# A decoder layer's opening redrawn, later quarter sums moved two steps, and weight halves kept in DRAM

## The chip, the core and the metric

The kernel runs on one core of one Trainium2 chip. The time is the device time in microseconds (us) of one execution, launch to end; the figures are medians of a few runs.

The engines: TensorE (PE) multiplies matrices, VectorE (DVE) and GpSimd (POOL) do elementwise work and sums, ScalarE (ACT) does copies, squares and exponentials, and SyncE (SP) issues nearly all DMAs, one after the other, in an order written out by hand. Each engine has its own instruction stream; semaphores tie them.

## The reference

One decoder layer on x (4 x 256 x 512) with a context of 4 x 1601 x 512, in float32:

```python
x = layernorm(x + self_attn(x))        # attention over the 16 positions inside a row, 8 groups
x = layernorm(x + cross_attn(x, ctx))  # 32 heads, 8 key heads, head size 128, 1857 keys
x = layernorm(x + ffn(x))              # router softmax over 64 experts, the top 8, expert biases

# self_attn: for each of the 1024 rows by itself
q, k, v = x @ Wq + bq, x @ Wk + bk, x @ Wv + bv      # (16, 32), (16, 8), (16, 8)
out[d, h] = sum_e softmax_e(sum_h q[d, h] k[e, h // 4] / 4) v[e, h // 4]

# cross_attn: kv = concat([ctx, x]); q and k are RMS-normed and scaled by a learned weight
p = softmax(q @ k.T / sqrt(128)); out = concat_heads(p @ v) @ Wo
```

## The kernel before

**Cross-attention.** There are 4 batches and 8 key heads, so 32 units (`UNITS`, batch-major). A unit has two halves: 512 query columns (2 heads of 256 rows) against 15 key tiles (`NJ`) of 128 keys. A *step* is one key tile of one half; a unit is a *cycle* of 30 steps (`CYCLE`). Products of which float32 accuracy is wanted are made of three passes over operands split in a high and a low part (`three`, L772 to L774): a weight chunk comes into `w_stage` by DMA, ACT copies the high part (`split` of ACT, L1184), and POOL subtracts it from the chunk for the low part (`split` of POOL, L746). Each unit needs five chunks of 128 x 1024: `Wkv`, `Wq` twice and `Wo` twice. They depend on the key head alone, so each batch does the same splits over again. `splits(s)` says at which step a chunk is split; `weights(chunk)` on SP loads a chunk two steps after the chunk two places ahead of it was split, and waits for that split's semaphore `s_wl`.

All engines walk through the same steps in the order of `for s in STEPS`, each in its own stream. At step s PE does the scores of tile s, then the *fill* jobs of that step, then P V of tile s - 20. Fill jobs: X turns a row tile of keys (transpose; ACT and DVE write its two halves, SP stores it in `kvT_scratch`), KV projects a key tile with `Wkv`, Q projects queries, KT and QT turn keys and queries, MT, AT and RB serve maxima and sums, O multiplies by `Wo`. DVE keeps the running maximum (L1364), which the scores of two steps on wait for, shifts the scores (L1348), and drains the jobs. ACT copies scores (L1047) and takes exponentials (L1060, L1061), and POOL writes `P_lo` (L689) and adds the probabilities up (L707). A negative step number is the opening, whose jobs stand in the table `OPENING`; the first scores are step 0.

**Self-attention.** Its 1024 rows are 8 tiles. PE turns and projects all eight in the opening (`SELF_AT`: "turn", "project"; L878, L889, L890). Tiles 0 and 1 are finished there, since batch 0's queries and last keys need their result (X 0 and X 1). The products are made in four quarters, quarter 0 by DVE and 1 to 3 by POOL (L459, L466), and summed by DVE (L1247, L1274). Tiles 0 and 1 go through five stages, "products", "scores", "normalise", "residual", "layernorm", both tiles at the same step one after the other, so DVE does a stage for tile 0 and at once for tile 1. Tiles 2 to 7 are kept in DRAM and finished later (`LATER`): each has 14 events, three in every 15 steps. At an event POOL makes one quarter's products in the one buffer `self_products`, and DVE sums that quarter at the end of the step after it (L1299 for q k, L1317 for p v), in its own order behind the other work of the step. The next quarter's product waits until the sum is done. The last of these tiles ends in unit 14 of 32.

**Order in the opening.** PE at a step: scores, fill jobs, then the self-attention's turn and projection, then P V. ACT likewise does the self-attention's copies last. SP loads one key row tile ahead of two weight chunks at the start.

## Time and profile before

| | |
|---|---|
| median of 3 runs | 2921.55 us (2919.27 to 2922.64) |
| the profiled execution | 2920.32 us, of which the span from first to last instruction 2918.5 |
| PE busy | 2791.9 us (96% of the span) |
| POOL busy | 2428.4 us (83%) |
| DVE, ACT busy | 2164.7 us (74%), 2066.0 us (71%) |
| mean granted PE clock | 0.978 |
| DMA | 364.81 MB, 125 GB/s |

### The profile page before, as it was taken

The numbers are of one execution on the slowest core, as the hardware profiler recorded it, in microseconds if no ns is written. First come the engines' busy times: TensorE is split into PE (matmuls) and PEld (weight loads), VectorE is DVE, ScalarE is ACT, GpSimd is POOL, SyncE is SP. The second block draws the span as 40 slices with busy tenths as digits, with TensorE's granted clock in tenths as the row PEclk, the third lists the DMA queues.
The fourth block names the chain that finished last, engine by engine and source line by source line (L and its number), as shares of the span: only waits on it lengthen the run. The fifth ranks groups of instructions, "written<-read, shape, count | busy, mean of one in ns | idle before, by whom it ended". The sixth has DMA issues, their size and how long they took to land. (4 is left out here: it accounts for less than half of the span.)

```text
span 2918.5 us, 46903 instructions
## 1 busy us (share of the span) xinstructions
PE 2791.9 (96%) x14860; PEld 2228.7 (76%) x14860; DVE 2164.7 (74%) x3483; ACT 2066.0 (71%) x3867; POOL 2428.4 (83%) x2283
## 2 busy tenths in 40 slices
PE   6999999999999999999999999999999999999976
PEld 4767787777777777778888888888888888888744
DVE  4667787777787778777777777777777777777755
ACT  3666777777676777777777777777777777777741
POOL 4488899889888999898888888888888888888880
PEclk9999999999999999999999999999999999999985
DMA  5633443333343434343444434334334333333201
GB/s 194 202 116 116 137 138 127 133 128 120 126 137 131 140 120 139 124 132 127 135 141 141 133 125 151 127 129 131 131 113 140 105 127 113 110 115 105 65 8 69
DMA packets 155604, 364.81 MB, mean 125 GB/s; under 512 B 12761, under 2 KB 48091, under 8 KB 155360
## 3 DMA queue, kind: packets, MB, share of 16 engines
q1 hardware_dynamic: 153608, 359.98, 37.1%
q8 instruction: 121, 1.98, 0.3%
q10 hardware_dynamic: 1752, 1.84, 0.2%
q14 instruction: 123, 1.01, 0.1%
HBM read 323.89 MB, written 37.88 MB: 124 GB/s over the span
## 5 line engine op out<-in xcount | busy, mean ns | idle before, releaser
L707 POOL TENSOR_TENSOR acc<-acc,scores 128x512 f32<-128x512 f32 (+1 forms) x832 | 1110.3, 1334 | 92.0 <-ACT scores L1061 51.8
L1364 DVE SCALAR_TENSOR_TENSOR running_max<-S_ps,rk,running_max 128x512 f32<-128x512 f32 (+1 forms) x896 | 668.8, 746 | 222.7 <-ACT scores L1047 216.6
L689 POOL TENSOR_TENSOR P_lo<-scores,P_hi 128x512 fp32r<-128x512 f32 x512 | 674.6, 1318 | 168.2 <-ACT scores L1061 168.0
L1047 ACT ACTIVATE scores<-S_ps,rk 128x512 f32<-128x512 f32 (+1 forms) x960 | 652.1, 679 | 200.9 <-PE S_ps L774 194.6
L1348 DVE TENSOR_TENSOR scores<-scores,Mb_ps 128x512 f32<-128x512 f32 (+1 forms) x960 | 648.4, 676 | 163.1 <-PE Mb_ps L922 163.1
L1061 ACT ACTIVATE scores<-scores 128x512 f32<-128x512 f32 (+1 forms) x960 | 596.6, 622 | 72.8 <-DVE scores L1348 71.7
L772 PE MATMUL S_ps<-QT_hi,KT_hi 128*128 128x512 f32 (+1 forms) x960 | 552.6, 576 | 27.0 <-DVE running_max L1364 24.0
L1060 ACT ACTIVATE P_hi<-scores 128x512 fp32r<-128x512 f32 x512 | 321.3, 628 | 263.8 <-DVE scores L1348 240.7
L774 PE MATMUL K_ps<-Wkv_hi,kvT 128*128 128x256 f32 (+1 forms) x1664 | 471.4, 283 | 0.0
L772 PE MATMUL K_ps<-Wkv_hi,kvT 128*128 128x256 f32 (+1 forms) x1664 | 470.6, 283 | 0.0
L773 PE MATMUL K_ps<-Wkv_lo,kvT 128*128 128x256 f32 (+1 forms) x1664 | 470.5, 283 | 0.0
L802 PE MATMUL OT_ps<-scores,V_full 128*128 128x512 f32 (+1 forms) x896 | 466.7, 603 | 0.0
L774 PE MATMUL S_ps<-QT_hi,KT_lo 128*128 128x512 f32 (+1 forms) x960 | 379.4, 395 | 0.0
L773 PE MATMUL S_ps<-QT_lo,KT_hi 128*128 128x512 f32 (+1 forms) x960 | 377.9, 394 | 0.0
L773 PEld LDWEIGHTS K_ps<-Wkv_lo,kvT 128*128 128x128 f32 (+1 forms) x1664 | 309.5, 186 | 19.5 <-issue 0.4
L772 PEld LDWEIGHTS K_ps<-Wkv_hi,kvT 128*128 128x128 f32 (+1 forms) x1664 | 309.3, 186 | 19.8 <-issue 0.5
L772 PEld LDWEIGHTS S_ps<-QT_hi,KT_hi 128*128 128x128 f32 (+1 forms) x960 | 178.0, 185 | 176.5 <-DVE running_max L1364 80.5
L774 PEld LDWEIGHTS K_ps<-Wkv_hi,kvT 128*128 128x128 f32 (+1 forms) x1664 | 309.7, 186 | 0.0
L773 PEld LDWEIGHTS S_ps<-QT_lo,KT_hi 128*128 128x128 f32 (+1 forms) x960 | 178.9, 186 | 119.1 <-issue 97.0
L772 PE MATMUL OT_ps<-P_hi,V_hi 128*128 128x512 f32 x512 | 219.0, 428 | 22.7 <-POOL P_lo L689 22.1
L774 PEld LDWEIGHTS S_ps<-QT_hi,KT_lo 128*128 128x128 f32 (+1 forms) x960 | 177.6, 185 | 45.6
L774 PE MATMUL OT_ps<-P_hi,V_lo 128*128 128x512 f32 x512 | 202.0, 395 | 0.0
(230 smaller groups left out, 5055.2 us busy)
## 6 DMA issues: line engine op xcount, KB each, us to landing
kvT<-kvT_scratch SPq DMA_DIRECT2D x403, 512.0 KB, 3.3
w_stage<-in_L_xattn_Wq SPq DMA_DIRECT2D x64, 512.0 KB, 4.2
w_stage<-in_L_xattn_Wo SPq DMA_DIRECT2D x64, 512.0 KB, 4.3
kvT_scratch<-built SPq DMA_DIRECT2D x45, 512.0 KB, 3.0
xrow<-in_ctx SPq DMA_DIRECT2D x48, 256.0 KB
w_stage<-in_L_xattn_Wk SPq DMA_DIRECT2D x32, 256.0 KB, 2.9
w_stage<-in_L_xattn_Wv SPq DMA_DIRECT2D x32, 256.0 KB, 3.2
kvT_scratch<-kvT SPq DMA_DIRECT2D x13, 512.0 KB, 3.7
```

Of the source, the lines that this page charges most:

```text
L689: e.tensor_tensor(P_lo[n % 2][0:r, :], prob(t)[0:r, :], f(P_hi[n % 2][0:r, :]), ALU.subtract)\
L707: e.tensor_tensor(a[0:r, :], a[0:r, :], prob(t)[0:r, :], ALU.add).then_inc(s_acc, 1)
L772: e.matmul(out, l_hi, r_hi, start=first, stop=False)
L773: e.matmul(out, l_hi, r_lo, start=False, stop=False)
L774: return e.matmul(out, l_lo, r_hi, start=False, stop=last)
L802: ins = e.matmul(OT_ps[:], V_full[v % 2][0:r, FULL.index(j), :], row[t % RING][0:r, :], start=first, stop=last)
L1047: e.activation(row[s % RING][0:r, :], S_ps[s % 2][0:r, :], ACT.Copy, scale=rk[0:r, v % 2, j:j + 1])\
L1060: e.activation(P_hi[n % 2][0:r, :], d, ACT.Exp)
L1061: e.activation(d, d, ACT.Exp).then_inc(s_p, 1)
L1348: e.tensor_tensor(d, d, Mb_ps[0:r, :], ALU.add).then_inc(s_d, 1)
L1364: e.scalar_tensor_tensor(a, src, k, a, ALU.mult, ALU.max).then_inc(s_top, 1)
```

## The change

Three parts, in one edit.

1. *The opening.* It begins at step -20 in place of -16. The jobs of `OPENING` get other steps; KV 10 goes from step -1 to 0 and the KV jobs behind it one step on, X 14 from -1 to 0, KT 3 from 5 to 6, QT 1 from 7 to 8. PE and ACT do the self-attention's jobs ahead of the fill jobs. SP loads self-attention row tiles 2 and 3 ahead of the second weight chunk. Tiles 0 and 1 no longer go through their stages together: the sums of the quarters are single entries of the order, tile 1 two steps behind tile 0.
2. *Quarter sums.* For tiles 2 to 7 the DVE sum of a quarter stands three steps after its product in place of one.
3. *Weight halves.* In batch 0 (units 0 to 7) SP stores both halves of each chunk in a DRAM scratch after the split. From unit 8 on there is no split: SP loads both halves from the scratch, at the steps of `reused(s)`, once the old contents have been used.

```diff
-    FIRST = -16
+    FIRST = -20
...
     OPENING = {
-        -16: [("X", 0, 2)],
-        -15: [("X", 0, 3)],
-        -14: [("X", 0, 4)],
-        -13: [("KV", 0, 0), ("X", 0, 5)],
...
-        -8: [("KV", 0, 5), ("KT", 0, 0), ("X", 0, 0), ("X", 0, 1)],
-        -7: [("Q", 0, 0, 0), ("Q", 0, 0, 1), ("X", 0, 10)],
-        -6: [("Q", 0, 1, 0), ("Q", 0, 1, 1)],
-        -5: [("KV", 0, 6), ("X", 0, 11)],
...
-        -2: [("KV", 0, 9), ("KT", 0, 1)],
-        -1: [("KV", 0, 10), ("QT", 0, 0), ("X", 0, 14)],
-        0: [("KV", 0, 11)],
...
+        -20: [("X", 0, 2)],
+        -19: [("X", 0, 3)],
+        -18: [("X", 0, 4)],
+        -17: [("KV", 0, 0)],
+        -16: [("KV", 0, 1)],
+        -15: [("X", 0, 5)],
+        -14: [("KV", 0, 2)],
+        -13: [("KV", 0, 3), ("X", 0, 6)],
+        -12: [("X", 0, 7)],
+        -11: [("KV", 0, 4), ("KT", 0, 0)],
+        -9: [("X", 0, 0), ("KV", 0, 5)],
+        -8: [("Q", 0, 0, 0), ("Q", 0, 0, 1)],
+        -7: [("X", 0, 1), ("X", 0, 8)],
+        -6: [("Q", 0, 1, 0), ("Q", 0, 1, 1), ("X", 0, 9)],
+        -5: [("KV", 0, 6), ("X", 0, 10)],
+        -4: [("KV", 0, 7), ("X", 0, 11)],
+        -3: [("KV", 0, 8), ("X", 0, 12)],
+        -2: [("KV", 0, 9), ("KT", 0, 1), ("X", 0, 13)],
+        -1: [("QT", 0, 0)],
+        0: [("KV", 0, 10), ("X", 0, 14)],
...
     def splits(s):
         if s < CYCLE_0:
-            chunk = {-16: ("Wkv", 0, 0), -15: ("Wq", 0, 0), -8: ("Wq", 0, 1), 1: ("Wkv", 1, 0), 4: ("Wq", 1, 0),
+            chunk = {-19: ("Wkv", 0, 0), -12: ("Wq", 0, 0), -11: ("Wq", 0, 1), 1: ("Wkv", 1, 0), 4: ("Wq", 1, 0),
...
-        return [chunk] if chunk and 0 <= chunk[1] < UNITS else []
+        return [chunk] if chunk and 0 <= chunk[1] < KVH else []
+
+    def reused(s):
+        v, c = divmod(s + AHEAD, CYCLE)
+        chunk = {5: ("Wkv", v + 1, 0), 11: ("Wq", v + 1, 0), 13: ("Wq", v + 1, 1), 14: ("Wo", v - 2, 1),
+                 24: ("Wo", v - 1, 0)}.get(c)
+        return [chunk] if chunk and KVH <= chunk[1] < UNITS else []
...
-        SELF_AT[[-15, -15, -13, -12, -11, -10, -9, -8][t]].append(("turn", t))
-        SELF_AT[[-14, -13, -12, -11, -10, -9, -8, -7][t]].append(("project", t))
-    for t in range(TPB):
-        for k, part in enumerate(("products", "scores", "normalise", "residual", "layernorm")):
-            SELF_AT[-13 + k].append((part, t))
+        SELF_AT[[-20, -20, -17, -16, -15, -14, -13, -12][t]].append(("turn", t, 0))
+        SELF_AT[[-19, -18, -16, -15, -14, -13, -12, -10][t]].append(("project", t, 0))
+    SELF_AT[-18] += [("products", 0, 0)]
+    SELF_AT[-17] += [("products", 1, 0), ("qk sum", 0, 0), ("qk sum", 1, 0)]
+    SELF_AT[-16] += [("qk sum", 0, 1), ("qk sum", 0, 2), ("qk sum", 0, 3), ("max", 0, 0)]
+    SELF_AT[-15] += [("exp", 0, 0), ("qk sum", 1, 1), ("normalise", 0, 0)]
+    SELF_AT[-14] += [("qk sum", 1, 2), ("qk sum", 1, 3), ("max", 1, 0)]
+    SELF_AT[-13] += [("exp", 1, 0), ("pv sum", 0, 0), ("normalise", 1, 0)]
+    SELF_AT[-12] += [("pv sum", 0, 1), ("pv sum", 0, 2), ("pv sum", 0, 3)]
+    SELF_AT[-11] += [("residual", 0, 0)]
+    SELF_AT[-10] += [("rsqrt", 0, 0)] + [("pv sum", 1, i) for i in range(4)] + [("layernorm", 0, 0)]
+    SELF_AT[-9] += [("residual", 1, 0)]
+    SELF_AT[-8] += [("rsqrt", 1, 0), ("layernorm", 1, 0)]
...
-            LATER[at[i] + 1].append(("qk sum", t, i))
+            LATER[at[i] + 3].append(("qk sum", t, i))
             LATER[at[6 + i]].append(("pv", t, i))
-            LATER[at[6 + i] + 1].append(("pv sum", t, i))
+            LATER[at[6 + i] + 3].append(("pv sum", t, i))
...
+            def store_halves(chunk):
+                kind, v, a = chunk
+                e.wait_ge(s_wh, W_AT[chunk] + 1)
+                e.wait_ge(s_wl, W_AT[chunk] + 1)
+                for i, half in enumerate(halves(chunk)):
+                    e.dma_start(whd[v, KINDS.index((kind, a)), :, i, :], f(half)).then_inc(halves_stored(chunk)[0], 16)
+
+            def load_halves(chunk):
+                kind, v, a = chunk
+                if kind == "Wkv":
+                    done = s_wk[v % 2]
+
+                    e.wait_ge(s_kt, NJ * (v - 1))
+                elif kind == "Wq":
+                    done = s_wq
+
+                    e.wait_ge(s_qf, 2 * v)
+                else:
+                    done = s_wo
+
+                    e.wait_ge(s_ff, F_AT["O", 2 * v + a - 1, 1] + 1)
+                e.wait_ge(*halves_stored((kind, v % KVH, a)))
+                for i, half in enumerate(halves(chunk)):
+                    e.dma_start(f(half), whd[v % KVH, KINDS.index((kind, a)), :, i, :]).then_inc(done, 16)
...
-                for n, chunk in enumerate(CHUNKS):
-                    if n >= 2 and W_STEP[CHUNKS[n - 2]] + 2 == s:
-                        weights(chunk)
+                for chunk in splits(s - 2):
+                    n = W_AT[chunk] + 2
+                    if n < len(CHUNKS):
+                        weights(CHUNKS[n])
+                    store_halves(chunk)
+                for chunk in reused(s):
+                    load_halves(chunk)
```

PE waits for the loaded halves in place of `s_wl` from unit 8 on, and ACT's `split` waits until the halves in the buffer that it writes have been stored.

## Rows read from the trace of the kernel before

**Rows 1.** Busy us of each engine by stage (instructions), granted clock, DMA share

```profile
0.00:92.60 92.60, 69.47 (x352) 49.95 (x353) 45.50 (x80) 30.59 (x61) 33.43 (x37) 0.96 0.58 193
...
162.10:1396.60 1234.50, 1189.55 (x6383) 954.10 (x6382) 949.95 (x1523) 895.87 (x1685) 1085.60 (x1012) 0.99 0.39 129
1396.60:2065.40 668.80, 667.28 (x3653) 541.83 (x3652) 509.11 (x800) 510.54 (x953) 584.56 (x553) 1.00 0.40 135
...
2763.00:2852.00 89.00, 65.04 (x214) 39.70 (x213) 47.01 (x68) 42.67 (x73) 70.99 (x54) 0.88 0.04 12
```

**Rows 2.** The same windows, one for each half unit of scores (64 halves)

```profile
121.41:162.10 40.69, 35.71 (x200) 28.67 (x199) 30.58 (x47) 28.91 (x55) 33.51 (x32) 0.99 0.53 177
...
645.41:692.38 46.97, 43.06 (x232) 34.53 (x231) 35.11 (x55) 33.20 (x62) 44.41 (x39) 0.98 0.42 135
692.38:734.37 41.99, 41.99 (x224) 33.42 (x224) 31.73 (x56) 30.49 (x60) 33.79 (x35) 0.98 0.35 118
...
1354.42:1396.59 42.17, 41.99 (x232) 34.29 (x231) 33.35 (x51) 33.65 (x63) 37.35 (x35) 1.00 0.46 145
...
1563.46:1604.77 41.31, 41.31 (x227) 33.50 (x226) 30.39 (x49) 30.32 (x59) 36.45 (x37) 1.00 0.45 151
1604.77:1647.13 42.36, 42.17 (x232) 34.30 (x231) 33.36 (x52) 33.60 (x63) 36.61 (x34) 1.00 0.41 140
```

**Rows 3.** Waits: who for whom, us in total, times, longest

```profile
DVE self_small L1317 <- POOL self_products L466: 45.6, 22, 4.6
DVE self_small L1299 <- POOL self_products L459: 40.5, 18, 4.3
```

**Rows 4.** Timeline, 171 to 186 us: start, duration, engine, operation [idle before]

```profile
180.66 1.26 POOL L459 TENSOR_TENSOR self_products<-self_qkv 128x512 f32<-128x512 f32 x1
...
181.95 0.69 DVE L1299 TENSOR_REDUCE self_small<-self_products 128x64 f32<-128x512 f32 x1 [4.11 <-POOL self_products L459]
...
183.95 0.50 PE L772 MATMUL S_ps<-QT_hi,KT_hi 128*128 128x512 f32 x1 [2.59 <-DVE running_max L1364]
```

**Rows 5.** Groups of instructions by form: count, busy us, mean ns, idle before

```profile
L746 POOL TENSOR_TENSOR Wo_lo<-w_stage,Wo_hi 128x1024 fp32r<-128x1024 f32 x64 | 154.4, 2412 | 22.5 <-ACT Wo_hi L1184 22.5
```

**Rows 6.** Timeline of the opening, by engine

```profile
9.69 2.29 DVE L1233 TENSOR_REDUCE scores<-scores 128x512 f32<-128x2048 f32 x1
...
10.54 1.08 PE L869 MATMUL F_ps<-ident,xrow 128*128 128x128 f32 x4 [10.54 <-DMA xrow<-in_ctx]
18.52 2.82 PE L889 MATMUL OT_ps<-scores 128*128 128x384 f32 x8
...
22.78 4.21 POOL L459 TENSOR_TENSOR scores<-scores 128x512 f32<-128x512 f32 x3 [2.46 <-ACT scores L1003]
37.84 11.45 POOL L466 TENSOR_TENSOR scores<-scores 128x512 f32<-128x512 f32 x6 [5.32 <-DVE scores L1262]
...
53.90 1.09 PE L869 MATMUL F_ps<-ident,xrow 128*128 128x128 f32 x4 [4.16 <-DVE kvT L1421]
54.78 4.96 PE L889 MATMUL Mb_ps<-scores,acc 128*128 128x384 f32 x8
...
90.86 0.47 PE L772 MATMUL S_ps<-QT_hi,KT_hi 128*128 128x512 f32 x1 [1.19 <-DVE QT_lo L1431]
```

**Rows 7.** Timeline of the end of the cross-attention, by engine

```profile
2807.97 2.35 POOL L746 TENSOR_TENSOR Wo_lo<-w_stage,Wo_hi 128x1024 fp32r<-128x1024 f32 x1
...
2813.28 0.50 PE L772 MATMUL OT_ps<-P_hi,V_hi 128*128 128x512 f32 x1 [4.76 <-POOL P_lo L689]
...
2839.38 1.06 ACT L1184 ACTIVATE Wo_hi<-w_stage 128x1024 fp32r<-128x1024 f32 x1 [4.18 <-PE F_ps L774]
...
2843.46 0.50 PE L772 MATMUL F_ps<-Wo_hi,OT_hi 128*128 128x512 f32 x1 [3.74 <-DVE OT_lo L1453]
```

**Rows 8.** DMA issues by line: count, KB each, median us from issue to landing

```profile
kvT<-kvT_scratch SPq DMA_DIRECT2D x403, 512.0 KB, 3.3
...
w_stage<-in_L_xattn_Wo SPq DMA_DIRECT2D x64, 512.0 KB, 4.3
```

More of the change, by code:

```diff
@@ L343, in attention @@
         F_ps = [ps(f"F_ps{i}") for i in range(2)]
-        sa_x = [sem(f"self_rows_loaded{i}") for i in range(2)]
+        sa_x = [sem(f"self_rows_loaded{i}") for i in range(4)]
         sa_qs = [sem(f"self_qkv_stored{i}") for i in range(2)]
@@ L373, in attention @@
         sa_d1 = sem("self_qk_products_of_DVE")
-        sa_sc = sem("self_scores_summed")
+        sa_sc = [sem(f"self_scores_summed{t}") for t in range(TPB)]
         sa_mx = sem("self_row_max")
@@ L382, in attention @@
         sa_d2 = sem("self_pv_products_of_DVE")
-        sa_o = sem("self_outputs_summed")
+        sa_o = [sem(f"self_outputs_summed{t}") for t in range(TPB)]
         sa_h = sem("self_residual_added")
@@ L399, in attention @@
         s_wl = sem("weights_lo")
+        s_ws = {"Wkv": [sem(f"Wkv_halves_stored{i}") for i in range(2)],
+                "Wq": [sem(f"Wq_halves_stored{i}") for i in range(2)],
+                "Wo": [sem(f"Wo_halves_stored{i}") for i in range(2)]}
+        s_wk = [sem(f"Wkv_halves_loaded{i}") for i in range(2)]
+        s_wq = sem("Wq_halves_loaded")
+        s_wo = sem("Wo_halves_loaded")
         s_xr = [sem(f"key_rows_loaded{i}") for i in range(2)]
@@ L437, in attention, with halves, halves_stored @@
         block = ctx.enter_context(nc.Block())
+        def halves(chunk):
+            kind, v, a = chunk
+            if kind == "Wkv":
+                return [x[v % 2][:].rearrange("p c n -> p (c n)") for x in (Wkv_hi, Wkv_lo)]
+            if kind == "Wq":
+                return [x[:, 2 * a:2 * a + 2, :].rearrange("p c n -> p (c n)") for x in (Wq_hi, Wq_lo)]
+            return [x[:].rearrange("p c n -> p (c n)") for x in (Wo_hi, Wo_lo)]
+        def halves_stored(chunk):
+            kind, v, a = chunk
+            if kind == "Wkv":
+                return s_ws[kind][v % 2], 32 * (v // 2 + 1)
+            return s_ws[kind][a], 32 * (v + 1)
         def bank(table, label):
@@ L593, in _ @@
             load_rows(0, TPB)
-            for chunk in CHUNKS[:2]:
-                weights(chunk)
+            weights(CHUNKS[0])
             load_rows(0, TPB + 1)
@@ L598, in _ @@
             load_self(3)
+            weights(CHUNKS[1])
             for s in STEPS:
                 v, c = divmod(s + AHEAD, CYCLE)
-                for part, t in SELF_AT[s - 1]:
+                for part, t, _ in SELF_AT[s - 1]:
                     if part == "layernorm":
@@ L755, in _ @@
                     split(chunk)
-                for part, t in SELF_AT[s]:
+                for part, t, _ in SELF_AT[s]:
                     if part == "products":
@@ L952, in _ @@
                     scores(s)
+                for part, t, _ in SELF_AT[s]:
+                    if part == "project":
+                        self_project(t)
+                for part, t, _ in SELF_AT[s]:
+                    if part == "turn":
+                        self_turn(t)
                 for x in fill(s):
@@ L1191, in _ @@
                     copy_OT(last // NJ)
+                for part, t, _ in SELF_AT[s]:
+                    if part == "exp":
+                        self_exp(t)
+                    elif part == "rsqrt":
+                        self_rsqrt(t)
+                for part, t, _ in SELF_AT[s]:
+                    if part == "project":
+                        self_copy_qkv(t)
+                for part, t, _ in SELF_AT[s]:
+                    if part == "turn":
+                        self_copy(t)
                 for kind, v in rooted(s - 2):
@@ L1336, in later, with opening_self @@
                     e.tensor_scalar(b_x[:], b_x[:], mv[:, 0:1], rs[:, 4:5], ALU.subtract, ALU.mult).then_inc(sb_x1, 1)
-            SELF_STAGE = {"products": self_products, "scores": self_scores, "normalise": self_normalise,
-                          "residual": self_residual, "layernorm": self_layernorm}
+            def opening_self(part, t, i):
+                if part == "products":
+                    self_products(t)
+                elif part == "qk sum":
+                    self_qk_sum(t, i)
+                elif part == "max":
+                    self_max(t)
+                elif part == "normalise":
+                    self_normalise(t)
+                elif part == "pv sum":
+                    self_pv_sum(t, i)
+                elif part == "residual":
+                    self_residual(t)
+                elif part == "layernorm":
+                    self_layernorm(t)
             def shift(t):
```

91 lines of the change are left out of this document (50 added, 41 removed), and 12 rows, old and new, of the table OPENING.

## The prediction, made before the changed kernel had run

> **What bounds the kernel now.** I read the windows by stage first [rows 1]: the reader sees that from 1396.6 us on TensorE (PE) is busy 667.28 of 668.80 us, at full clock. There the kernel stands on PE alone, and nothing taken from another engine can shorten it. Three stretches are not like that: the opening (69.47 busy of 92.60), the stretch from 162.1 to 1396.6 (1189.55 of 1234.50), and the last 89 us before the feed-forward (65.04 busy).
>
> The windows by half give the price of the middle stretch [rows 2]. The two undisturbed halves take 41.31 and 42.36 us, a pair 83.67. The 28 halves from 162.1 to 1396.6 would take 14 x 83.67 = 1171.4 at that pace; they take 1234.5. The excess is 63.1 us. It is the stretch in which the self-attention of row tiles 2 to 7 ("later") is threaded through, and it ends when that ends.
>
> The waits name the place [rows 3]: VectorE (DVE) waits 45.6 + 40.5 = 86.1 us, 40 times, for a quarter's products of GpSimd (POOL). The timeline shows one [rows 4]: POOL, already behind with a weight split, starts the product at 180.66; the quarter sum starts at 181.95 after 4.11 us of idle DVE; PE, which needs the running maximum that DVE owes, starts its scores at 183.95 after 2.59 us of idleness.
>
> **Quarter sums later.** Nothing is removed: 48 sums of 0.69 us run two steps later, at the end of step +3 in place of +1. A step is 41.84/15 = 2.79 us, so the allowance grows by 5.58 us; the longest of the waits is 4.6 [rows 3]. All forty should vanish. The next product of POOL still finds its sum done: it stands four steps or more after the last one, and behind two POOL operations that need a DVE result of its own step. The sums now fall partly into steps where DVE drains O or RB results or subtracts OT_lo; that costs DVE 0.7 us in a step whose result PE needs a step later. I put it in what remains.
>
> What remains is read from halves with no quarter wait. Six such halves last 254.7 us in all (the first and the last, at 692.38 and 1354.42, stand in [rows 2]), where the undisturbed pace gives 251.0: 0.6 us each. Over 28 halves 17 us stay, so 63.1 - 17 = 46 us come back. The half at 121 us has two more such waits, and PE is idle for 5 of its 40.69 us [rows 2]; I count 3 of them, which the POOL term below takes back. POOL gets fuller: the heaviest half has 44.41 us of POOL work [rows 2], above the 42.36 us that the half will last, so POOL falls behind by some 2 us there. P_lo is read by PE about two and a half steps (7 us) after the exponential, so 1.3 for its own duration leaves some 4 to 5 us of cover; I take 3 us for places where it doesn't do, and the two terms of 3 cancel. Sum: **46 us**, bounds 30 (POOL gives back a third) and 66 (all of it).
>
> **Weight halves stored.** For units 8 to 31 the 24 x 5 = 120 splits go: 120 x 2.4 = 288 us of POOL [rows 5], and as many Copies of ScalarE at 1.06 [rows 7]. From 1396.6 to 2727 that buys nothing: PE has 1.5 us idle in 669 [rows 1]. In the later half of the self-attention stretch it takes 2.5 x 2.4 = 6 us from each half of POOL, which is why I don't charge more for POOL's load. In exchange SP issues 80 stores of 512 KB in units 0 to 7 (40 MB) and 240 loads of 512 KB in place of 120 (or two of 256) from the weights. The stores stand behind the wait for POOL that the next weights load had already at that place, so no new wait stands before the kvT loads. They put 1 MB and 0.5 MB of weights ahead of a kvT load. The opening moved 193 GB/s at a busy share of 0.58 [rows 1], which makes 333 at full share: 1.5 MB take 4.5 us, and a kvT load lands in 3.3 [rows 8]. A kvT buffer is free some five steps (14 us) before its use. Hidden, 0 us; if the cover were gone, up to 5 us each.
>
> The end does gain. From 2763 PE has little left and POOL works 70.99 of 89.00 us [rows 1], without a gap before 2834; PE waits for its P_lo (4.76 us in one place, right behind the split at 2807.97) [rows 7]. Two splits stand in that chain: 4.8 us off. The last Wo half is different. Before, its raw data was there, and Copy (from 2839.38) and split hid beside the end of the chain to 2843.46. Now the load itself can only start when the O product before is done, at 2839.3, and two DMAs of 512 KB follow: 4.3 us for one [rows 8], 1.5 for the second one's bytes, so 2845, some 1.6 us later. Net **3 us**, bounds 0 and 5.
>
> The Trainium skill (DMA: Bandwidth & Descriptors, Anatomy of one DMA) gives a fixed cost of about 2.0 us and 436 GB/s behind it, which would make the two loads 4.4 us together, an estimate; the row with 4.3 us for one is what the trace has, and the rule would only add 1 us to the gain at the end.
>
> **The opening.** PE starts at 10.54 and gives the first score at 90.86 [rows 6]: 80.3 us, with 68 of work, so 12 idle; behind an idle stretch of 4.16 that ends at 53.90 the eight matmuls of a projection took 4.96 us in place of 2.82 (the slower of the two clock levels, 1.2 GHz), and 2.7 us were lost with their neighbours. Work is the same after, except that KV 10 (1.5 us) and X 14 (0.5) go behind the first score.
> Step by step: the row tiles are turned before X 2, so the projection of tile 0 waits only for DVE's sum of Wq, 9.69 + 2.29 + 0.66 = 12.6, six us before the 18.52 of now. PE then has its chain of projections (3.6 us each, 2.8 for the eight matmuls and 0.8 for the bias) with X and KV between. POOL does its first split at 20 (ScalarE copies after X 3), so tile 0's products start at 22.7, where they are now. But tile 0 now goes alone: sums by 29, exp behind ScalarE's copies at 31, values by POOL 32.5 to 38.2, residual at 46; ScalarE reaches its rsqrt at 54, X 0 can be turned at 56, when the eighth projection ends (56.4). The second tile's rsqrt stands behind KV 5's copies (59.2), and DVE drains X 0 only behind layernorm(1), so the queries wait from 58.4 to 61.5. From there PE has about 18 us of work to the score: with 1.5 us for the last QT drain, **82**, or 84 with the tile ring: X 8 to X 13 follow each other in 2 us each, moving 768 KB each, above 333 GB/s, so slips of 1 to 2 us.
> That is 7 to 9 us earlier, less the 2 moved behind: 5 to 7. I take **5**, bounds 13 (all idle time gone) and -3 (the new idle stretch at 58 lowers the clock as the one at 50 did, and the ring of tiles waits for stores).
>
> DVE and POOL beside each other: three products take 4.21 us, six value products, beside DVE operations of two inputs, 11.45 (1.91 each) [rows 6]. I counted 1.9 for values. The Trainium skill (SBUF: State Buffer, SBUF: two separate sides) says a DVE operation with two SBUF inputs and a POOL operation lock each other out of a shared port pair. By this rule the interleaved sums, with one input, cost POOL nothing, and by the rows the sum is the same.
>
> **Sum.** 46 + 3 + 5 = 54. The profiled execution took 2920.32 (span 2918.5 and 1.8 around it), 1.2 below the median of 2921.55. So 2866 for its own and 2867 for the median; I say **2867**.
>
> **Rivals.** (1) *POOL takes DVE's place.* For it: POOL is busy 1085.60 of 1234.50 [rows 1], in a stretch of some 1188 us that is 91%, and event products, splits of units below 8 and newton steps fall together in one half (44.41). If PE waits for P_lo by half of what the heavy halves exceed, and what DVE lost stays lost in a third of the places: 30 us back, 2920 + 1 - 38 = 2883. Against: POOL idles for ScalarE's results even now, and units from 8 on lose 6 us a half.
> (2) *Everything comes back*, the residual too, since it is a clock that had fallen after the waits (the mean of the stretch is 0.99) and POOL's relief: 60 + 5 + 10 = 75: 2847. For: windows just behind a waiting half show lower clocks. Against: quiet halves at clock 1.00 are still up to 1 us long.
> (3) *Slower.* The stores and loads on SP's one queue make a kvT tile late. Place: the kvT load behind a chunk's store pair, 40 chunks in units 0 to 7 and 120 loads later. Price: 14 us of cover against 4.5 + 3.3; it decides if the queue behind runs at under 150 GB/s; then 1.5 MB take 10 us, and 2 us lost at half of the 160 places cost 160 x 0.5 x 2 = 160 less 54: 3027; at a tenth of them, no change. Against: mean DMA share 0.39 in that stretch.
> (4) *No effect of the later sums*, because the DVE wait only shows POOL's lateness and the two steps move DVE's work into full steps: only 3 + 5 remain, 2913.
>
> **How the numbers follow.** Mine 0.68, (1) 0.17, (2) 0.08, (4) 0.03, (3) 0.04, of which nearly all slower. The likeliest value is 2867. Its own range is the sum of half the bounds, 2855 to 2880; to hold 8 in 10 it reaches over (1) and most of (2): 2848 to 2888. About 0.2% (6 us) is what a measurement of this kernel can tell from no change. Faster 0.94, same 0.02, slower 0.04.
>
> **What would show it.** Quarter sums with next to no wait for POOL; halves of 41.5 to 43 us from 162 us on, with PE over 99% busy; no change in the undisturbed halves (83.7 a pair); the first score at 82 to 84; POOL at about 73% busy in place of 87% beyond unit 8; the end from 2763 shorter by 3. Wrong if PE shows waits for P_lo in the heavy halves, for kvT anywhere, or if the first score comes no earlier than 90.

## The result: 2846.8 us in place of 2921.5

The changed kernel took 2846.84 us (median of 4 runs, 2846.22 to 2848.53), beside 2921.49 of the kernel before: a ratio of 0.9746, 95% interval [0.9729, 0.9763], 75 us. I had said 2867 and a range from 2848; it came out 1 us below the range. The sign and the main cause were right; how much came back was not.

The halves of the scores (0 to 63, each from one first running maximum to the next) show where. Forecast and measured, from the two profiled executions (spans 2918.5 and 2845.6 us):

| stretch | before | after | difference | forecast |
|---|---|---|---|---|
| up to half 2 (opening, halves 0 and 1) | 162.10 | 162.75 | +0.65 | -5, and -3 in half 1 |
| halves 2 to 29 (later self-attention) | 1234.5 | 1171.8 | -62.7 | -46 in all, with the 3 of half 1 |
| halves 30 to 61 (undisturbed) | 1331.0 | 1323.8 | -7.2 | 0 |
| half 62 to the end of the span | 190.9 | 187.3 | -3.7 | -3 |

Windows by stage of the changed kernel, columns as in [rows 1] (its code is longer: a line of before stands 34 to 100 lines further down):

```profile
0.00:91.87 91.87, 71.08 (x332) 50.04 (x333) 47.34 (x80) 29.89 (x60) 32.43 (x37) 0.95 0.68 229
...
162.75:1334.52 1171.77, 1165.33 (x6383) 945.44 (x6382) 946.01 (x1522) 862.42 (x1645) 1004.89 (x978) 1.00 0.54 183
1334.52:2693.20 1358.68, 1358.03 (x7417) 1103.00 (x7415) 1022.49 (x1629) 973.35 (x1860) 1006.33 (x1054) 1.00 0.45 154
```

In the middle stretch PE is now busy 1165.33 of 1171.77 us, 99.5%, where it was 1189.55 of 1234.50. So of the 62.7 us 38.5 are idle time of PE, and 24.2 are busy time: the same 6383 matmuls ran faster, at a granted clock of 1.00 in place of 0.99. From half 30 on POOL is busy 74% (1006.33 of 1358.68); I had said 73. Windows of single halves:

```profile
91.87:126.75 34.88, 31.59 (x183) 27.34 (x182) 18.40 (x29) 20.77 (x39) 9.18 (x13) 0.90 0.69 246
126.75:162.75 36.00, 34.89 (x200) 28.83 (x199) 29.97 (x46) 29.42 (x57) 30.17 (x30) 1.00 0.71 242
...
625.02:667.39 42.37, 42.17 (x232) 34.28 (x231) 35.64 (x55) 31.15 (x60) 35.19 (x34) 1.00 0.65 214
667.39:708.40 41.01, 41.01 (x224) 33.10 (x223) 32.23 (x58) 29.69 (x59) 35.30 (x36) 1.00 0.41 148
...
1334.52:1375.36 40.84, 40.84 (x223) 33.10 (x222) 28.94 (x48) 28.66 (x56) 29.84 (x33) 1.00 0.39 133
```

Half 13, at 625.02, took 46.97 before, the heaviest of all, and half 14 behind it 41.99 [rows 2]; they take 42.37 and 41.01 now. Half 1 is down from 40.69 to 36.00. Half 0 is the exception: 34.88, against 28.80 before, at a granted clock of 0.90. The waits say the same, by [rows 3]: of 86.1 us of quarter waits, one of 0.7 is left (second line). Of PE's waits for P_lo (first line) 3.8 us lie in halves 2 to 29, as before the change (3.9), and 12.6 in the end.

```profile
PE OT_ps L842 <- POOL P_lo L759: 16.8, 23, 2.6
...
DVE self_small L1386 <- POOL self_products L500: 0.7, 1, 0.7
```

And the place that [rows 4] showed, in its timeline: POOL's product starts at 181.75, not earlier than before (180.66), behind the same split; the sum, in DVE's order behind other work now, finds it just done.

```profile
179.41 2.38 POOL L816 TENSOR_TENSOR Wo_lo<-w_stage,Wo_hi 128x1024 fp32r<-128x1024 f32 x1
181.75 1.29 POOL L500 TENSOR_TENSOR self_products<-self_qkv 128x512 f32<-128x512 f32 x1
...
183.07 0.69 DVE L1386 TENSOR_REDUCE self_small<-self_products 128x64 f32<-128x512 f32 x1
```

### The profile page after: what moved, and what is told of

Read it like the earlier page. It is cut to its first block and busy times, and to the rows that moved or that the text cites. A ratio compares the mean times of both kernels' runs of the same rounds, so it can differ in the third digit from the quotient of the medians.

```text
span 2845.6 us, 46879 instructions
## 1 busy us (share of the span) xinstructions
PE 2766.7 (97%) x14860; PEld 2224.4 (78%) x14860; DVE 2144.0 (75%) x3483; ACT 1965.3 (69%) x3747; POOL 2147.4 (75%) x2163
## 3 DMA queue, kind: packets, MB, share of 16 engines
q8 instruction: 121, 1.98, 0.3%
## 5 line engine op out<-in xcount | busy, mean ns | idle before, releaser
L842 PE MATMUL S_ps<-QT_hi,KT_hi 128*128 128x512 f32 (+1 forms) x960 | 559.3, 583 | 6.9 <-DVE running_max L1464 4.8
L872 PE MATMUL OT_ps<-scores,V_full 128*128 128x512 f32 (+1 forms) x896 | 459.2, 594 | 0.0
L1220 ACT ACTIVATE nat<-K_ps 128x256 f32<-128x256 f32 (+1 forms) x256 | 94.7, 370 | 158.8 <-PE K_ps L844 158.3
```

The costliest lines, as they stand in the source:

```text
L842: e.matmul(out, l_hi, r_hi, start=first, stop=False)
L872: ins = e.matmul(OT_ps[:], V_full[v % 2][0:r, FULL.index(j), :], row[t % RING][0:r, :], start=first, stop=last)
L1220: e.activation(nat[q // 2 % 2][0:r, at:at + k, :], src[0:r, 0:k, 0:HD], ACT.Copy).then_inc(s_kc, 1)
```

## The experiments

Twelve kernels, each timed against the kernel before on the same chip. All compute the whole layer. The median of the kernel before was 2917.31 beside E1 to E4, 2918.60 beside E5 to E8, 2921.25 beside E9 to E11 and 2918.55 beside E12. The first maximum, the start of half 2 and the stretches are read from one profiled execution of each, in us; "end" is half 62 to the end of the span. They don't add up to the medians: E1's profiled execution was its fastest (2858.03), and its stretches are 62 us below those of before, where the medians differ by 57.

| kernel | median | ratio [95%] | first maximum | half 2 starts | 2-12 | 13-29 | 30-61 | end |
|---|---|---|---|---|---|---|---|---|
| before | | 1 | 92.61 | 162.10 | 483.3 | 751.2 | 1331.0 | 190.9 |
| changed | 2846.84 | 0.9746 [0.9729, 0.9763] | 91.87 | 162.75 | 462.3 | 709.5 | 1323.8 | 187.3 |
| E1 sums only | 2860.48 | 0.9802 [0.9789, 0.9816] | 91.58 | 156.39 | 461.0 | 717.6 | 1331.2 | 190.1 |
| E2 halves only | 2890.23 | 0.9907 [0.9894, 0.9921] | 95.96 | 167.68 | 482.6 | 729.3 | 1323.8 | 184.7 |
| E3 opening only | 2920.41 | 1.0006 [0.9997, 1.0015] | 92.35 | 163.46 | 481.8 | 751.2 | 1330.9 | 191.8 |
| E4 sums and halves | 2847.44 | 0.9759 [0.9746, 0.9772] | 96.27 | 163.04 | 460.8 | 709.5 | 1323.8 | 187.0 |
| E5 E4, stores later | 2845.21 | 0.9749 [0.9736, 0.9763] | 92.22 | 161.11 | 462.6 | 709.4 | 1323.8 | 187.0 |
| E6 changed, stores later | 2844.76 | 0.9751 [0.9737, 0.9764] | 92.73 | 163.43 | 461.0 | 709.5 | 1323.8 | 187.6 |
| E7 E1, Wo split moved | 2853.40 | 0.9776 [0.9763, 0.9790] | 92.91 | 157.74 | 461.5 | 716.0 | 1323.8 | 192.3 |
| E8 E4, sums at +2 | 2847.60 | 0.9758 [0.9745, 0.9771] | 96.36 | 164.86 | 462.7 | 709.5 | 1323.8 | 186.9 |
| E9 E4, stores from unit 2 | 2843.53 | 0.9732 [0.9719, 0.9746] | 92.49 | 157.32 | 461.0 | 711.8 | 1323.8 | 186.7 |
| E10 changed, layer norm later | 2842.32 | 0.9730 [0.9716, 0.9743] | 85.61 | 158.75 | 461.1 | 709.4 | 1323.8 | 187.2 |
| E11 E10, E9's stores, earlier splits | 2840.47 | 0.9724 [0.9711, 0.9737] | 87.13 | 152.84 | 461.0 | 711.8 | 1323.8 | 187.0 |
| E12 E10 and E9's stores | 2838.24 | 0.9732 [0.9718, 0.9745] | 88.59 | 154.22 | 460.9 | 712.7 | 1323.8 | 186.6 |

**E1, the quarter sums alone.**

```diff
-            LATER[at[i] + 1].append(("qk sum", t, i))
+            LATER[at[i] + 3].append(("qk sum", t, i))
...
-            LATER[at[6 + i] + 1].append(("pv sum", t, i))
+            LATER[at[6 + i] + 3].append(("pv sum", t, i))
```

> The kernel before with the quarter sums alone moved from step +1 to +3; opening and weight splits as before. Theory A (the late sums carry the whole excess of the middle stretch by themselves): about 62 us less than before, 2859 to 2862, with the 28 halves from 162 us on at the pace of the undisturbed ones, odd halves beyond 1396 still 42.36. Theory B (the weight halves' relief of POOL is needed too, and P_lo or the residual of quiet halves remains without it): 30 to 50 us less, 2872 to 2892, with the missing time in halves 13 to 29 and waits of PE for P_lo there.

It gave 57 us (1.98% of 2917.31, the median of before on its chip). The time, 2860.48, is in theory A's range, and the gain some 5 us short of it. Halves 2 to 29 fall by 56.0, half 1 by 4.7:

```profile
156.39:1334.90 1178.51, 1167.12 (x6383) 946.03 (x6382) 950.07 (x1522) 895.26 (x1684) 1092.46 (x1014) 1.00 0.41 136
```

Before, PE was busy 1189.55 of 1234.50 us there at 0.99 [rows 1]. So 33.6 us of the 56.0 are idle time, and 22.4 are busy time of the same 6383 matmuls. Before, the granted clock was below 1.00 in twelve of these halves (lowest 0.93, half 18); in E1 it is 1.00 in all. Its mean was 0.986 to three places, from which I estimate 17 of the 22.4 us. The waits had cost twice: PE stood idle, and then it ran at the lower level for a while.

What is missing stands in halves 13 to 29: 717.6 in place of the changed kernel's 709.5. Two halves of E1, and one undisturbed odd half:

```profile
617.35:660.97 43.62, 42.16 (x232) 34.33 (x231) 35.52 (x55) 33.98 (x63) 39.94 (x36) 1.00 0.42 134
...
786.08:830.19 44.11, 42.74 (x234) 34.39 (x233) 36.98 (x55) 33.52 (x63) 40.29 (x37) 1.00 0.42 134
...
1459.41:1501.74 42.33, 42.15 (x232) 34.33 (x231) 33.36 (x52) 33.56 (x63) 36.56 (x34) 1.00 0.43 140
```

The first two are halves 13 and 17, PE idle for 1.5 and 1.4 us; with stored halves they last 42.4 and 42.3. PE's waits for P_lo come to 4.5 us in seven places of halves 13 to 29, and to 0.6 in three with stored halves. So a part of theory B is true: POOL's relief is needed for 8 us, no more.

**E2, the weight halves alone** (part 3 of the change on the kernel before).

> The kernel before with the weight halves stored in batch 0 and loaded from unit 8 on; opening and sums as before. Theory A (the 0.44 us of each odd half beyond 1396 and the end come from here, and the middle stretch hardly changes since its waits follow the order, not POOL's load): 16 x 0.44 + 3.6 = 11 us, and up to 5 more in the middle: 2905 to 2911. Theory B (POOL without splits is early enough for the quarter sums at +1 too, beyond unit 8): the waits shrink in the later 13 of the 28 halves, 15 to 30 us more: 2880 to 2896. Rival of both: stores on the one DMA queue cost in units 0 to 7, 3 us or more longer there.

27 us (0.93%), theory B's lower end. Halves 13 to 29 fall by 21.9, halves 30 to 61 by 7.2, the end by 6; the opening and halves 0 and 1 pay 5.6. Halves 2 to 12 pay nothing for their stores (482.6 against 483.3). The quarter waits are shorter, but by far not gone:

```profile
DVE self_small L1387 <- POOL self_products L495: 36.4, 20, 4.6
DVE self_small L1369 <- POOL self_products L488: 34.7, 16, 4.3
```

71 us of 86 are left, and yet 22 us came back in those seventeen halves, where the quarter waits fell from 48.5 to 33.6. E1 and E2 overlap: 33.6 and 21.9 in halves 13 to 29 by themselves, 41.7 together, so 13.8 us are counted in both. The medians say the same: 56.8 + 27.1 - 69.9 = 14.0.

**E3, the opening alone** (part 1).

> The kernel before with the redrawn opening alone. Theory A (the opening as such is worth next to nothing, its 2 us of moved work and a lower clock take what the order gains): 0 to 2 us less, 2919.5 to 2921.5, first running maximum at 91 to 92. Theory B (the stores of weight halves load the DMA engines from 55 us on and cost the opening what it would gain): without them the first maximum at 87 to 89 and 3 to 6 us less in all, 2916 to 2919.

No difference (1.0006, interval [0.9997, 1.0015]). The first maximum comes 0.3 us earlier and half 2 starts 1.4 later. Theory B fell: without any stores the redrawn opening is no earlier than with them.

**E4, sums and halves with the old opening** (parts 2 and 3).

> The changed kernel with the old opening: late quarter sums and stored weight halves. Theory A (the opening is worth nothing): 2846 to 2849, the time of the changed kernel within 2 us. Theory B (the opening gives the 5 us that I forecast, and something else gave more): 2851 or more. If sums and halves each alone sum up to it, they are independent; if this one is faster than the sum, one needs the other.

Theory A: the changed kernel's time without its opening, as far as two ratios with overlapping intervals can say. But the way there differs: the first maximum is at 96.27, 4.4 us behind the changed kernel, and halves 0 and 1 take 66.8 in place of 70.9. The new opening stands the stores better, and its halves give that back.

**E5 and E6, the opening's stores at steps 0 to 2**, with the old and the new opening:

```diff
                 for chunk in splits(s - 2):
...
-                    store_halves(chunk)
+                    if s - 2 >= 0:
+                        store_halves(chunk)
+                if 0 <= s < 3:
+                    store_halves(CHUNKS[(1, 2, 0)[s]])
```

> Old opening, late sums, stored halves, but the stores of the three chunks that are split in the opening stand at steps 0, 1 and 2, where the DMA engines showed a busy share of 0.1 to 0.4. Theory A (the 3.7 us by which the first maximum comes later with stored halves than without, 96.27 against 92.61 and 91.58, is key rows arriving late behind these 3 MB of stores): first maximum back at 91 to 93, third half at 157 to 159, 4 to 6 us less than with the stores in the opening: 2841 to 2844. Theory B (it is the order of the issues or the second lot of stores in units 0 and 1): no change, 2846 to 2849, or the first half gets longer by what the opening gains.

> The changed kernel with the same three chunks' stores at steps 0, 1 and 2. Theory A (the redrawn opening already carries the stores without loss, first maximum 91.87 with them and 92.35 without; what it gained for the stores is lost in the first half at the low clock): first maximum 91 to 92, third half no earlier than 159, time 2843 to 2847, that is 1 to 3 us slower than the old opening with late stores. Theory B (the stores' load is what kept the new opening from its 82 to 84 us): first maximum at 88 or before and 2840 or less.

E5: the first maximum is back at 92.22 (theory A), but halves 0 and 1 take 68.9, 2.1 more than in E4; half 2 starts at 161.11, only 1.9 earlier and outside theory A's 157 to 159. The stores had brought half 0 to a DMA share of 0.96, from 0.80 in E4. Of the 2.1 us, 1.6 are PE's busy time for the same matmuls, at a granted clock of 0.98 and 0.97 where E4 had 1.00, and 0.6 a longer wait for key rows. E6: nothing moved beyond what two executions differ by; the new opening does not wait for stores.

**E7, one split moved**, on E1:

```diff
-            chunk = {5: ("Wkv", v + 1, 0), 11: ("Wq", v + 1, 0), 15: ("Wo", v - 2, 1), 19: ("Wq", v + 1, 1),
+            chunk = {5: ("Wkv", v + 1, 0), 11: ("Wq", v + 1, 0), 17: ("Wo", v - 2, 1), 19: ("Wq", v + 1, 1),
```

> Late sums alone, and the split of each unit's second Wo chunk two steps later, behind the newton steps. Theory A (the 0.44 us in each odd half beyond 1396 us is P_lo behind this split and five newton operations on POOL): odd halves 41.92 in place of 42.34, even ones unchanged, 16 x 0.42 = 7 us there and some 4 more before 1396: 2849 to 2854. Theory B (DMA or PE order makes the odd halves longer): odd halves unchanged at 42.3, 2858 to 2862.

Theory A, to the tenth: halves 30 to 61 fall from 1331.22 to 1323.84, what stored halves give. The same half as E1's last above:

```profile
1459.32:1501.24 41.92, 41.92 (x232) 34.27 (x231) 33.31 (x51) 33.12 (x62) 36.23 (x34) 1.00 0.39 132
```

The wait that went was POOL's P_lo behind the split and five newton operations. In E1 between 1400 and 2600 us, the waits of the weight load (engine, line, waited for, us in total, times, longest):

```profile
PEld OT_ps L772 <- POOL P_lo L689: 6.4, 15, 0.5
```

6.4 us in 15 places is 0.43 each, the 0.41 by which an odd half got shorter. The 4 us more that I expected ahead of half 30 did not come (halves 2 to 29 fell by 1.0), and the end is 2.2 us longer than E1's, which no run explains.

**E8, sums at +2** in place of +3, on E4.

> Old opening, stored halves, quarter sums at step +2 in place of +3. Theory A (what counts is the allowance: the waits at +1 are 2.15 us in the mean and 4.6 at most, a step adds 2.79, so only the longest fifth stay): 2 to 8 us slower than at +3, 2849 to 2856, with 5 to 10 quarter waits of under 2 us. Theory B (a threshold, POOL's product never done within a step's time): half or more of the 50 us is lost, 2870 or more.

Neither: the same time as E4 (2847.60), while DVE's waits are far from gone:

```profile
DVE self_small L1387 <- POOL self_products L495: 16.1, 8, 3.4
DVE self_small L1369 <- POOL self_products L488: 16.0, 10, 3.2
```

Of these 32 us in 18 waits, 10.4 in six waits of up to 2.7 lie in halves 13 to 29 and cost nothing there: 709.5 us in both, PE idle for 1.1 in both. The other 21.8, up to 3.4 long, lie in halves 1 to 12, and there the profiled execution is 3.6 us longer than E4's. What fits is that a wait of DVE that ends before PE asks for the running maximum is free; one step of allowance more was already enough for nearly all.

**E9, stores from unit 2 on:** units 0 and 1 store nothing, units 8 and 9 split once more and store in their place.

```diff
-        return [chunk] if chunk and 0 <= chunk[1] < KVH else []
+        return [chunk] if chunk and 0 <= chunk[1] < KVH + 2 else []
...
             def store_halves(chunk):
                 kind, v, a = chunk
+                if v < 2:
+                    return
```

> Old opening, late sums, stored halves, but units 0 and 1 store nothing: units 8 and 9 split once more and store in their place, so 6 MB of stores leave the opening and the first two halves. Theory A (with stored halves the opening and halves 0 and 1 end 6.65 us later than with late sums alone, 163.04 against 156.39, and all of it is the load of the stores): third half at 156 to 158, ten more splits in units 8 and 9 cost 0.44 us in two halves and little more; 5 us less than with stores from unit 0: 2841 to 2844. Theory B (the next weights' place in the queue behind the stores or something else costs it): third half at 161 or later, 2845 or more.

Theory A: half 2 starts at 157.32, near E1's 156.39 and 5.7 us ahead of E4; the ten splits cost 2.3 us in halves 13 to 29. Much of what the stores did in E4 was to make key rows late, 3.2 us of the 5.7; from 75 us to the first maximum E4 also ran at a granted clock of 0.92 where E9 had 1.00. PE's waits for key rows before 163 us, E4, and then E9:

```profile
PE F_ps L933 <- DMA xrow<-in_ctx: 17.1, 4, 9.8
```

```profile
PE F_ps L936 <- DMA xrow<-in_ctx: 13.9, 2, 10.3
```

**E10, one entry of DVE's order** in the changed kernel:

```diff
-    SELF_AT[-8] += [("rsqrt", 1, 0), ("layernorm", 1, 0)]
+    SELF_AT[-8] += [("rsqrt", 1, 0)]
+    SELF_AT[-7] += [("layernorm", 1, 0)]
```

> The changed kernel with one entry of VectorE's order moved: tile 1's layer norm at step -7 in place of -8, so that X 0 is drained while ScalarE's rsqrt of tile 1 is still due. Theory A (the redrawn opening loses its gain between X 0 and the queries: 2.84 us idle and nine matmuls of 0.63 us at the low clock behind it): queries start at 61.5 in place of 64.54, no low clock, first maximum at 87 to 89, 2843 to 2845 in all since what follows keeps its waits. Theory B (the tile ring and the key rows that SP fetches in order are what sets the score's time): queries earlier, but the first maximum stays at 91 to 92, 2846 to 2848.

Theory A, and more: the time is 2842.32, and the first score at 83.43, where I had forecast 82 to 84 for the change itself. The trace of it, by engine:

```profile
59.39 0.68 DVE L1522 TENSOR_TENSOR xT<-F_ps,xT 128x512 fp32r<-128x512 f32 x1
...
57.20 0.66 PE L946 MATMUL F_ps<-ident,scores 128*128 128x128 f32 x4 [1.93 <-DVE scores L1379]
...
60.13 0.50 PE L843 MATMUL K_ps<-Wq_hi,xT 128*128 128x512 f32 x1 [0.84 <-DVE xT L1522]
...
83.43 0.51 PE L843 MATMUL S_ps<-QT_hi,KT_hi 128*128 128x512 f32 x1 [1.66 <-DVE QT_lo L1532]
```

X 0 is drained at 59.39, ahead of the layer norm, and the queries start at 60.13 behind 0.84 us of idleness. The edit did not bring all of the 6.3 us at the first maximum: 0.9 were there before the moved entry (X 0 is turned at 57.20, in the changed kernel at 58.11), and the clock stayed up here from 55 to 75 us (1.00, in the changed kernel 0.83), which it did not in E12 with the same entry moved. 4.0 us are left at half 2; this opening still carries the early stores, and PE waits 3.5 us for one key row tile behind the first score, where the changed kernel waits 1.6.

**E11 and E12, both edits together**, E11 with Wq's first splits one step earlier as well:

```diff
-            chunk = {-19: ("Wkv", 0, 0), -12: ("Wq", 0, 0), -11: ("Wq", 0, 1), 1: ("Wkv", 1, 0), 4: ("Wq", 1, 0),
+            chunk = {-19: ("Wkv", 0, 0), -13: ("Wq", 0, 0), -12: ("Wq", 0, 1), 1: ("Wkv", 1, 0), 4: ("Wq", 1, 0),
```

> The changed kernel with the layer norm of tile 1 a step later, both splits of unit 0's Wq one step earlier (-13 and -12: POOL stood idle for 5.78 us before them and then stretched a newton step of VectorE from 0.16 to 2.26 us), and stores from unit 2 on. Theory A (three independent losses of the new opening, all to be had back): X 0 at 56, queries at 60, first maximum at 85 to 87, third half at 154 to 156, 2839 to 2842: the fastest of all. Theory B (halves 0 and 1 take back what the opening gains, as they did in every run with this opening, because the moved jobs and key rows set their pace): first maximum at 85 to 88, but third half not before 158, 2843 or more.

> The changed kernel with the layer norm of tile 1 a step later and stores from unit 2 on, Wq's splits where the change puts them. Theory A (the earlier splits cost 1.5 us by standing in front of tile 1's values on POOL and stretching a residual add of VectorE from 0.68 to 2.38 us; without them the opening is that of the run with the layer norm alone, and halves 0 and 1 are those without early stores, 65.7): first maximum at 85.6, third half at 151 to 152, 2838.5 to 2840. Theory B (the halves take back what the opening gains): third half at 152.8 or later, 2840.5 or more.

Halves 0 and 1 take 65.7 in both, 5 to 7 us less than with early stores, and half 2 starts 8 to 10 us ahead of the changed kernel. E11's theory A holds for the time (2840.47) and half 2 (152.84, earlier than its 154 to 156), but its earlier splits bought nothing at X 0, which came at 58.51, beside 58.68 in E12 without them; see the last section. E12 should have had its first maximum at 85.6; in the execution profiled it had it at 88.59, with the granted clock at 0.79 to 0.87 from 55 to 75 us where E10 had 1.00. So its half 2 starts at 154.22, in theory B's range, while its median is just below theory A's. By the medians the two are the lowest here, 6 to 8 us under the changed kernel. By the ratios (0.9724 and 0.9732, against 0.9732 in E9, 0.9730 in E10 and 0.9746 in the changed kernel, each against before on its own chip) all five intervals overlap: which of them is fastest is not shown.

## Why the prediction was right in direction and too small in size

**Quarter sums.** The mechanism held: with them alone the waits of [rows 3] shrink from 86.1 us to 0.3, and no price for a next product or for DVE's fuller steps appears. The size was wrong, and the step that failed is "over 28 halves 17 us stay". I took 0.6 us a half from six of the halves without a quarter wait and charged it to all. With the sums alone (E1) 7.1 us stay: 1178.5 against 1171.4 by the undisturbed pace. E1 also shows where. Nine halves have no such wait (5, 7, 10, 14, 19, 21, 24, 28, 29): they took 382.0, at the undisturbed pace 377.0, and take 381.2 in E1. Their residual is their own, and the later sums leave it. The nineteen others went from 852.5 to 797.3, with 794.3 by the undisturbed pace: 3.0 us stay there, 0.16 a half and not 0.6. The stored halves took most of the rest: in the changed kernel the nine take 378.4 and the nineteen 793.3, together 1171.8, the undisturbed pace of before within 0.4. Part of that is the 0.44 us by which odd halves got shorter everywhere (below): by the changed kernel's own undisturbed pace, 41.31 and 41.92, the 28 halves would take 1165.2, so 6.6 us stay by that measure. Beside the 46 that I forecast with half 1 stand 60.7 us in E1 (56.0 and 4.7) and 67.4 in the changed kernel, about the bound of 66 that I had written for "all of it".

The clock stood only in rival (2). PE was idle for 45.0 of the 1234.5 us; a good part of the 63.1 us stood in its busy time, which fell by 22.4 in E1, and came back with the waits.

**POOL's load.** I charged 3 us for P_lo in heavy halves. With the splits left in (E1) PE's waits for P_lo in halves 2 to 29 go from 3.9 to 7.5 us, about what I charged; with stored halves they are 3.8. That the stored halves take another 8 us from halves 13 to 29 on top of the later sums, and that the two parts overlap by 14, I saw only as "why I don't charge more". Rival (1), in which only 30 us come back, is dead.

**The undisturbed halves.** "Hidden, 0 us" was wrong by 7.2. I argued from PE's idle time, 1.5 us in 669 [rows 1]. But the odd half had 42.36 with 42.17 busy [rows 2]: 0.19 idle, and a loss of 0.44, since the weight load had waited 0.43 and the matmuls behind it were spread. E7 shows the cause by itself.

**The end.** Forecast -3, measured -3.7. The terms: half 62 took 0.8 less, which I had not counted; from the last first maximum to the last Wo half's Copy or load it took 76.1 before and 70.8 now, 5.3 less (I said 4.8); from there to PE 4.1 and 5.1, 1.0 more (I said 1.6); and the feed-forward behind took 1.5 more. The long wait for P_lo is 2.64 in place of 4.76 [rows 7]:

```profile
2738.74 0.50 PE L842 MATMUL OT_ps<-P_hi,V_hi 128*128 128x512 f32 x1 [2.64 <-POOL P_lo L759]
...
2764.01 0.32 SPq L606 DMA_DIRECT2D Wo_hi<-weight_halves_scratch  x1
2764.37 0.43 SPq L606 DMA_DIRECT2D Wo_lo<-weight_halves_scratch  x1
...
2769.08 0.76 PE L842 MATMUL F_ps<-Wo_hi,OT_hi 128*128 128x512 f32 x1 [4.66 <-DMA Wo_lo<-weight_halves_scratch]
```

From the first issue at 2764.01 to the matmul at 2769.08 the two loads took 5.07 with the step to PE, where I had 5.8 from rows. By the fixed cost and the rate that the Trainium skill (DMA: Bandwidth & Descriptors, Anatomy of one DMA) gives they would have taken 4.4, an estimate; the section gives them for DMAs issued by GpSimd, and these were issued by SyncE.

**The opening.** Forecast -5, measured nothing (E3), and +0.65 up to half 2 against a half 1 that the sums shorten by 4.7. X 0 came 2 us later than forecast (56, and 58.11), and from there the walk went astray. The timeline of the changed kernel, by engine:

```profile
52.61 4.66 POOL L816 TENSOR_TENSOR Wq_lo<-w_stage,Wq_hi 128x1024 fp32r<-128x1024 f32 x2 [5.78 <-ACT Wq_hi L1267]
...
55.02 2.26 DVE L38 TENSOR_TENSOR scores<-scores 128x1 f32<-128x1 f32 x1
...
58.11 1.11 PE L945 MATMUL F_ps<-ident,scores 128*128 128x128 f32 x4 [1.93 <-DVE scores L1378]
...
61.74 0.38 ACT L1220 ACTIVATE nat<-K_ps 128x256 f32<-128x256 f32 x1 [1.88 <-PE K_ps L844]
...
62.28 0.20 ACT L1092 ACTIVATE scores<-scores 128x1 f32<-128x1 f32 x1
...
62.75 0.16 DVE L36 SCALAR_TENSOR_TENSOR scores<-scores 128x1 f32<-128x1 f32 x1 [2.36 <-ACT scores L1094]
...
63.80 0.68 DVE L1521 TENSOR_TENSOR xT<-F_ps,xT 128x512 fp32r<-128x512 f32 x1
...
64.54 0.52 PE L842 MATMUL K_ps<-Wq_hi,xT 128*128 128x512 f32 x1 [2.84 <-DVE xT L1521]
...
66.13 0.63 PE L843 MATMUL K_ps<-Wq_lo,xT 128*128 128x512 f32 x1
...
71.81 0.50 PE L842 MATMUL K_ps<-Wq_hi,xT 128*128 128x512 f32 x1 [1.79 <-DVE xT L1521]
...
78.38 0.39 PE L842 MATMUL K_ps<-Wkv_hi,kvT 128*128 128x256 f32 x1 [1.23 <-DVE kvT L1521]
...
83.51 0.39 PE L842 MATMUL K_ps<-Wkv_hi,kvT 128*128 128x256 f32 x1 [1.14 <-DVE kvT L1521]
...
89.43 0.77 PE L842 MATMUL S_ps<-QT_hi,KT_hi 128*128 128x512 f32 x1 [1.66 <-DVE QT_lo L1531]
```

The first 2 us are, for the most part, DVE's newton step of tile 0 (a few operations of one element a row that make the layer norm's factor), 2.26 in place of 0.16, beside POOL's splits (last section); I had costed the interleaving for POOL alone. Then ScalarE does tile 1's rsqrt at 62.28, behind KV 5's copies, where I had 59.2. DVE waits for it 2.36 us in its order, and X 0's drain, long possible, stands behind it until 63.80. I had seen this wait and put the queries at 61.5; they start at 64.54, 2.84 us of PE's idleness before them. What I had not put in the sum is what comes of it: eight query matmuls at 0.61 to 0.63 us where the upper clock level gives 0.40. After that come two slips of the tile ring (1.23 and 1.14, forecast 1 to 2 in all) and drains that cost 1.79 and 1.66, where I had 1.5 for one. The reason that I had written beside the bound of -3, "the new idle stretch at 58 lowers the clock as the one at 50 did", was what happened in this execution, though E3's 0 is above that bound. E10 takes one of these waits away and has its first score at 83.43, in an execution in which the clock stayed up.

Behind the first score there is a second loss. The granted clock at the start of half 0:

```profile
91.87:95.87 4.00, 4.00 (x20) 3.71 (x19) 1.18 (x2) 0.80 (x2) 0.00 (x0) 0.53 0.03 13
95.87:99.87 4.00, 4.00 (x32) 3.79 (x31) 1.94 (x4) 3.03 (x6) 0.70 (x1) 1.00 0.29 118
```

At 0.53, about the lower level of 1.2 GHz, PE does 20 matmuls in 4 us and 32 in the next 4. Halves 0 and 1 of the changed kernel are 4.1 us longer than E4's: PE is busy 4.8 us more in half 0 (31.59 against 26.75), and its waits are 0.7 shorter. E12 has the same jobs there at a granted clock of 1.00, and PE is busy for 27.90: so 3.7 of the 4.8 are the clock's, and the other 1.1 are the KV and X work moved there.

**Stores.** No kvT load was late, rival (3) is dead, and kvT's landing went from 3.3 to 3.7 us only. What did get late were key rows in the opening and in halves 0 and 1: 3.2 us of the 5.7 that early stores cost with the old opening (E4 against E9). I had looked for the cover of kvT, five steps, and not for that of the key rows, which have two tiles of ring and no more.

**The sum** of the four stretches is -72.9. Rival (2), everything comes back, had 2847 as its time. Its reason, that the residual was in part a clock that had fallen after the waits and in part POOL's load, is what E1 and the changed kernel show. The 10 us of the opening in it did not come, and the 7 us of the undisturbed halves stood in no case: that it hit the time is in part luck.

## What to carry to other kernels

A bound beside a term ("all of it: 66") deserves its chance: before a residual is charged, ask whether the places that wait have it too. Here it was measured where nothing waited (0.5 us a half, and it stayed with the sums alone), while the nineteen halves with waits kept 0.16. A wait can also cost more than its idle time: 22 of E1's 56 us came back as busy time, at a clock that no longer fell. When a wait is moved in one engine's written order, list what stands behind the waiting instruction there, and who waits for that; one layer norm ahead of one drain kept PE idle for 2.84 us in place of 0.84. An idle engine in the trace is not the measure of what a wait costs: 10.4 us of DVE's waits cost nothing in halves 13 to 29 of E8, and 0.19 us of idleness cost 0.44 in each odd half.

## What the runs showed of the hardware

*DVE and POOL hold each other up in two-input work, and the one that comes second pays.* In the changed kernel's opening above a newton operation of one element a row, 0.16 us elsewhere, starts at 55.02 beside POOL's splits and takes 2.26: it ends at 57.28, and the splits, begun at 52.61 for 4.66, end at 57.27. E10 and E12 show the same operation at 2.27 and 2.26. The sums of one input just before it, four in 2.45 us beside the same splits, were not stretched. E11 moved the splits and moved the stretched operations with them:

```profile
47.94 2.37 POOL L820 TENSOR_TENSOR Wq_lo<-w_stage,Wq_hi 128x1024 fp32r<-128x1024 f32 x1 [11.04 <-ACT Wq_hi L1274]
50.28 4.90 POOL L508 TENSOR_TENSOR scores<-scores 128x512 f32<-128x512 f32 x3
55.13 2.35 POOL L820 TENSOR_TENSOR Wq_lo<-w_stage,Wq_hi 128x1024 fp32r<-128x1024 f32 x1
...
48.48 2.38 DVE L1372 TENSOR_TENSOR scores<-scores 128x512 f32<-128x512 f32 x1
...
55.81 1.68 DVE L36 SCALAR_TENSOR_TENSOR scores<-scores 128x1 f32<-128x1 f32 x1
...
58.51 0.66 PE L949 MATMUL F_ps<-ident,scores 128*128 128x128 f32 x4 [3.44 <-DVE scores L1385]
```

The residual add of 0.68 us takes 2.38 beside the first split, and a newton step that starts at 55.81 ends at 57.49 with the second (57.48). Each split takes its usual 2.35 to 2.37. The Trainium skill (SBUF — State Buffer, SBUF: two separate sides) says that a DVE operation with two SBUF inputs and one of POOL lock each other out of a shared port pair for a whole instruction, whoever starts first; the trace agrees. At the splits it was DVE that came second. The other way round, POOL pays: of the three value products at 50.28 the first meets the rest of the stretched residual add (to 50.86) and takes 1.99, the two behind it 1.54 and 1.50. In the opening of before, a value product that POOL starts at 41.87 while DVE is in one of its own (40.56 to 42.93) takes 2.44, against 1.51 for two beside sums; that is the 11.45 for six [rows 6]. The earlier splits also stood in front of tile 1's value products (50.28), which may be why X 0 came no earlier in E11 (58.51) than in E12 (58.68); no run has the one without the other.

*The same gap, two clocks.* Behind an idle stretch of 1.93 us X 0's four transposes took 1.11 us in the changed kernel and 0.66 in E10, and behind 1.95 us 1.11 in E12; behind 3.44 us in E11 it was 0.66. Whether the granted clock falls at such a place differs from kernel to kernel, perhaps from execution to execution; where it does, X 0 and the twelve key matmuls behind it take 3.6 us in place of 2.1 (the changed kernel against E10), and the twelve query matmuls 1.6 us more. That is the noise under any comparison of openings here.
